# First attention of a four-layer kernel: the mask of half of the transposed score tiles goes from TensorE to VectorE

## The reference, cut to what matters

```python
q = apply_rope(proj(Wq, bq)) * Dh ** (-0.5)      # 16 heads of 16
k = apply_rope(proj(Wk, bk))
v = proj(Wv, bv)
scores = jnp.einsum('bhqd,bhkd->bhqk', q, k)
rel = idx[None, :] - idx[:, None]
blocked = (rel > 0) | (rel < -WINDOW)            # WINDOW = 128
scores = jnp.where(blocked[None, None], -jnp.inf, scores)
probs = jax.nn.softmax(scores, axis=-1)
out = jnp.einsum('bhqk,bhkd->bhqd', probs, v)
```

## Time and profile before

| | |
|---|---|
| median of 3 runs | 2595.47 us (2590.16 to 2601.94) |
| the profiled execution's own time | 2598.99 us |
| its span, first to last instruction | 2597.1 us |
| mean granted PE clock over the span | 0.945 |
| busy share of the span: PE, DVE, ACT, POOL | 85%, 54%, 38%, 35% |
| first attention, about | 60 to 1075 us of the span |

### The profile page before, as it was taken

The page is one execution under the profiler, slowest core; times in us unless marked ns, Lnnn a source line. Parts: engine busy times, 40 slices in busy tenths (PEclk is TensorE's granted clock), DMA queues, the critical chain, the costliest instruction groups (busy, mean ns, idle before and its releaser), DMA issues.

```text
span 2597.1 us, 42566 instructions
## 1 busy us (share of the span) xinstructions
PE 2202.2 (85%) x17140; PEld 1379.6 (53%) x17140; DVE 1411.1 (54%) x2526; ACT 994.3 (38%) x1450; POOL 898.7 (35%) x573
## 2 busy tenths in 40 slices
PE   3899999999999999588787879999678888888885
PEld 1444555555555455366565637766455555555553
DVE  2445555555555554346454535444467776777672
ACT  0133333333333333245444433333235554554443
POOL 4122222222222220003121221012438777777785
PEclk7799999999999999789889989999889999999997
DMA  5555555555555551455776661011454454436411
GB/s 132 103 113 116 107 115 114 107 108 113 114 111 117 111 110 39 149 195 196 239 268 232 241 206 49 17 65 49 150 144 115 116 159 133 129 101 172 112 48 49
DMA packets 226386, 328.86 MB, mean 127 GB/s; under 512 B 14368, under 2 KB 163984, under 8 KB 225936
## 3 DMA queue, kind: packets, MB, share of 16 engines
q1 hardware_dynamic: 219200, 321.56, 47.3%
q10 hardware_dynamic: 6992, 4.60, 0.6%
HBM read 197.53 MB, written 127.93 MB: 125 GB/s over the span
## 4 chain that ended last, share of the span: by engine, by line
PE 28%; DVE 11%; POOL 6%; DMA 6%; ACT 3%; issue 3%; SPq 2%; ACTq 0%; DVEq 0%; POOLq 0%
DVE l1f_rowmax L1811 4%; PE l1a_slot L1411 4%; POOL l1f_added L1688 4%; PE l1a_slot L1402 2%; POOL l1f_added L1690 2%; PE l0f_slot L1112 2%; PE l1a_slot L1453 2%; PE l1f_slot L1942 2%; PE l1f_slot L1933 2%; PE l0f_slot L1119 2%; DMA l0f_wide<-expert_outputs 2%; DMA l0f_x<-x 2%; PE l1f_os L1866 2%; DMA expert_outputs<-l0f_wide 1%; SPq L879 1%
## 5 line engine op out<-in xcount | busy, mean ns | idle before, releaser
L534 ACT ACTIVATE l0a_probs<-l0a_slot 128x1024 f32<-128x1024 f32 (+1 forms) x256 | 248.4, 971 | 336.2 <-PE l0a_slot L694 189.1
L591 DVE TENSOR_REDUCE l0a_rowmax<-l0a_slot 128x4 f32<-128x1024 f32 (+1 forms) x256 | 293.5, 1156 | 128.7 <-PE l0a_slot L704 125.8
L1760 ACT ACTIVATE l1f_probs<-l1f_slot 128x1024 f32<-128x1024 f32 x240 | 243.8, 1022 | 270.2 <-PE l1f_slot L1942 262.5
L1688 POOL TENSOR_TENSOR l1f_added<-l1f_probs 128x1024 f32<-128x1024 f32 x117 | 277.3, 2370 | 155.6 <-ACT l1f_probs L1760 155.6
L1811 DVE TENSOR_REDUCE l1f_rowmax<-l1f_slot 128x1 f32<-128x1024 f32 x240 | 287.5, 1217 | 65.7 <-PE l1f_slot L1933 65.1
L494 POOL TENSOR_TENSOR l0a_turned<-l0a_turned 128x512 f32<-128x512 f32 x32 | 40.7, 1272 | 557.0 <-DVE l0a_turned L577 557.0
L1942 PE MATMUL l1f_slot<-l1f_Qs,l1f_Ks 128*128 128x256 f32 x960 | 173.1, 305 | 37.2 <-DVE l1f_lo L1801 14.8
L1933 PE MATMUL l1f_slot<-l1f_Ks,l1f_Qs 96*128 96x512 f32 x480 | 179.0, 458 | 25.5 <-DVE l1f_rowmax L1811 18.7
L1942 PEld LDWEIGHTS l1f_slot<-l1f_Qs,l1f_Ks 128*128 128x128 f32 x960 | 146.5, 198 | 94.5 <-DVE l1f_rowmax L1811 31.9
L694 PE MATMUL l0a_slot<-l0a_mask,l0a_ident 128*128 128x512 bf16 (+1 forms) x512 | 150.3, 376 | 25.0 <-issue 22.6
L636 PE MATMUL l0a_O<-l0a_probs,l0a_V 128*32 128x128 f32 x3840 | 156.5, 279 | 10.4 <-issue 10.4
(11 more groups left out here) (196 smaller groups left out, 3987.9 us busy)
## 6 DMA issues: line engine op xcount, KB each, us to landing
expert_outputs<-l0f_wide SPq DMA_DIRECT2D x64, 512.0 KB, 3.4
l0f_wide<-expert_outputs SPq DMA_DIRECT2D x32, 1024.0 KB, 11.5
l0a_Qs<-qk_rows SPq DMA_DIRECT2D x96, 256.0 KB, 7.6
l0a_Ks<-qk_rows SPq DMA_DIRECT2D x96, 256.0 KB, 14.5
l1f_Ks<-kq_rows SPq DMA_DIRECT2D x48, 512.0 KB, 8.5
l0f_f<-in_dram SPq DMA_DIRECT2D x10, 2048.0 KB, 15.7
qk_rows<-l0a_hi SPq DMA_DIRECT2D x32, 512.0 KB, 2.8
qk_rows<-l0a_lo SPq DMA_DIRECT2D x32, 512.0 KB, 4.2
```

What stands on the lines that cost most here:

```text
L534: exp_ready.by(act.activation(probs[:, t % 2, HG * g:HG * g + HG, 0:reach, :], s[:, :, 0:reach, :], ACT.Exp, scale=SCALE))
L591: max_ready.by(dve.reduce_max(rowmax[:, t, :, 2 * g:2 * g + 2], s[:, :, :, first:2 * P], AX))
L1688: halved.by(pool.tensor_tensor(added[:, u, :], probs[:, 0, u, :], probs[:, 1, u, :], ALU.add))
L1760: exp_done.by(act.activation(probs[:, half, u - FIRST[b], :], s[:, :], ACT.Exp, scale=SCALE))
```

## The change

In tr steps with an odd g the two mask matmuls are left out: four score matmuls alone fill the slot. DVE gets a new part in these steps: as soon as the scores are there it adds the mask table to them, in place in PSUM, in one instruction over 128 x 1024 elements (128 x 512 for a sequence's last tile), and raises the new semaphore `masked`. ACT's exponential of these steps waits for `masked` besides the scores. The slot's reader is still the exponential. Tr steps with an even g and all nat steps stay as they were.

```diff
+        masked = signal("masked", BT * NHG // 2)
 ...
                 if kind == "tr":                       # ACT
                     t, g = i // NHG, i % NHG
                     s = by_pair(arrived(act, X, step)).rearrange("p s j a q -> p (s j) a q")
-
+                    if i % 2:
+                        masked.wait(act, X, i // 2 + 1)
 ...
+                if kind == "tr" and i % 2:             # DVE
+                    s = by_pair(arrived(dve, X, step)).rearrange("p s j a q -> p (s j) a q")
+                    reach = 1 if n and i // NHG == BT - 1 else 2
+                    visible_from = maskT[:, 0:reach, :].unsqueeze(1).broadcast_to([P, HG, reach, P])
+                    masked.by(dve.tensor_tensor(s[:, :, 0:reach, :], s[:, :, 0:reach, :], visible_from, ALU.add))
 ...
-                    mask_ends = bool(kind == "tr" and g % 2)
+                    masked_here = not (kind == "tr" and g % 2)
 ...
-                    if not mask_ends:
-                        add_mask()
+                    if masked_here:
+                        for half in range(2):
+                            mm(o[:, half, :, reach, :], ident16[:, :], table[:, reach, :].unsqueeze(1).broadcast_to([P, 2, wide, P]),
+                               start=True, stop=False, skip_group_check=True)
                     for j in range(2):
 ...
-                                      right[r, 2 * g + j, moving], start=mask_ends and not j, stop=not mask_ends,
+                                      right[r, 2 * g + j, moving], start=not masked_here, stop=True,
                                       skip_group_check=True, tile_position=(HALF * half, 0))
-                    if mask_ends:
-                        last = add_mask()
```

More of the change, by code:

```diff
@@ L399, in window_attention_layer @@
         stacked = {w: signal(f"stacked_{w}", 6, 16) for w in "qk"}
-        max_ready = signal("max_ready", BT * NHG); maxT_ready = signal("maxT_ready", BT)
+        masked = signal("masked", BT * NHG // 2); max_ready = signal("max_ready", BT * NHG); maxT_ready = signal("maxT_ready", BT)
         placed = [signal(f"placed{t}", BT, 16) for t in range(2)]
@@ L555, in _ @@
             dve.memset(ln.half[:, :], -0.5).then_inc(setup, 1)
-            for s in (turned_ready, v_ready, max_ready, maxT_ready, recip_ready, ao_ready, summed):
+            for s in (turned_ready, v_ready, masked, max_ready, maxT_ready, recip_ready, ao_ready, summed):
                 s.start(dve)
@@ L689, in piece @@
                     wide = reach.stop - reach.start
-                    mask_ends = bool(kind == "tr" and g % 2)
-                    def add_mask():
+                    masked_here = not (kind == "tr" and g % 2)
+                    if masked_here:
                         for half in range(2):
[L694 to L697, removed]
-                    if not mask_ends:
-                        add_mask()
+                            mm(o[:, half, :, reach, :], ident16[:, :], table[:, reach, :].unsqueeze(1).broadcast_to([P, 2, wide, P]),
+                               start=True, stop=False, skip_group_check=True)
                     for j in range(2):
```

## The result

The changed kernel takes 2698.8 us (median of 4 runs, 2690.98 to 2705.56) against 2597.01 us for the kernel before (also 4 runs): a ratio of 1.040, 95% interval 1.0358 to 1.0441, +102 us. The prediction said 2680 us with a range of 2636 to 2713, slower. The profiled execution took 2704.77 us, its span is 2702.8 us.

A forecast was written before the change was run, and what follows sets the result against it. PE, working in list order, was taken to set the pace, waiting only at unread slots. 2599.0 + 60.5 (waits) + 24 (clock) = 2683.5 us, given as a median of 2680 us; range 2636 to 2713 us.

The forecast's parts named there:

- The removed work: 128 odd tr steps lose two mask matmuls each on PE; at most 53 us saved.
- The addition's price: One DVE addition in PSUM takes 1.22 us, from its likeness to the residual sum; outer end 2.14 us.
- The rival of a slow write to PSUM: Every DVE addition takes 2.14 us, as PSUM reading and writing take turns; 2738 us; chance 0.09.
- The waits: PE waits for late exponentials: 1.90, 0.30, 1.54, 0.04 us in quarters 3, 0, 1, 2; 60.5 us over 16 blocks.
- The clock: In quarters 1 and 3, 6 of 10 new PE pauses halve the clock, 1.25 us each; 24 us.
- The first rival: Pauses in quarters 1 and 3 too short or well placed to lower the clock; waits only, 2656 us; chance 0.30.
- the prediction's other sum: All new pauses in quarters 1 and 3 lower the clock, costing 40 us in place of 24.
- PE's columns decide: Rival: DVE and ACT finish before PE returns, exponentials under about 0.4 us late in quarters 1, 3; 2543 us; chance 0.06.
- a wash: In quarters 1 and 3 the addition passes earlier DVE work for half the delay; near 2595 us; chance 0.05.

The follow-up runs named there:

- six-additions: Against the changed kernel, DVE adds the mask in all odd tr steps except tr1 of quarters 1 and 3, which have it on PE; 2601.89 us.
- picked: Against the changed kernel, DVE adds the mask only for tr3 of quarters 0 and 1 and tr1 of quarter 2; 2589.96 us.
- kernel with fillers: The changed kernel plus matmuls of no use in PE's pauses of quarters 0, 1 and 3, waits untouched; 2650.39 us.
- quarters 1 and 3 filled: The changed kernel plus matmuls of no use in PE's pauses of quarters 1 and 3 only; 2672.87 us.
- kernel with two additions: Against the changed kernel, DVE adds the mask only for tr1 of quarters 1 and 3, all others on PE; 2705.25 us.

## Why the prediction was right, by its steps

- *The removed work.* Right in that almost none of the 53 us shows, because PE waits behind the pairs. Where no wait follows it does show: 0.53 us for one pair, tr3 of quarter 1, in the six-additions and picked kernels. That is this pair's own spacing (567.25 to 567.78 in the kernel before, shown above); the 0.44 us taken for all pairs was read at another step.
- *The addition's price.* 1.22 us taken, 1.226 measured. The rival of a slow write to PSUM is out.
- *The waits.* 1.54 predicted and 1.46 measured in quarter 1, 1.90 and 1.90 in quarter 3, with the clock held up. Quarter 0: 0.30 and 0.24; quarter 2: 0.28 and 0.13 in one kind of blocks, -0.2 and -0.45 in the other. The sum was 60.5 us; 54.2 us were measured in the kernel with fillers. In quarter 0 the way there was not the one predicted: ACT's list was not full, tr3 moved by 0.39 us and not by 0.74 (4.42 us after tr1 instead of 4.03), and its missing mask gave 0.30 back and not 0.44.
- *The clock.* This is the term that was mis-sized: 24 us predicted, 48 measured (101.8 - 54.2). The step let 6 of 10 pauses bring the clock down, at 1.25 us each, in quarters 1 and 3 alone. In fact 14 of 16 pieces of quarter 1 and 13 of 15 of quarter 3 hold a stretch at half clock. It is 6.8 us long in most pieces of quarter 1, twice the 3.3 us of the step, and 3.4 in quarter 3; by the medians it costs 3.28 - 1.46 = 1.82 us and 3.07 - 1.90 = 1.17 us. Quarter 0, which the step did not price, lost to the clock in six blocks. Over all pieces the changed kernel lies above the kernel with all fillers by 25 us in quarter 1, 17 in 3, 8 in 0 and 2 in 2, in one trace of each; the medians of their runs lie 48 us apart. The first rival, waits without the clock, would have given 2656 us; it is what the kernel with all fillers gives, 2650 us, so the clock is what stands between that rival and the result. The Trainium skill's "TensorE: Matmul & The Clock Gate", section "A second HAM failure mode: psum-queue depth-cycling", says that short pauses between groups of matmuls bring the clock down and cost throughput, without a price. With every pause counted by that rule, the prediction's other sum was 40 us; the measured 48 lie nearer to it than to 24.
- *PE's columns decide*, and *a wash*: not borne out in the changed kernel. The first fails at the point named for it: tr1's exponential starts 1.82 us (quarter 3) and about 3 us (quarter 1) later than before, counted from its scores. The second asked that the addition pass the work ahead of it, and it passes none: in quarters 1 and 3 it starts when the last pass over k and the normalisation end.
- The end: 2680 predicted, 2698.8 measured. The 18.8 us are 24 us too little for the clock and 6 us too much for the waits, with 1.5 us from the median of the kernel before. Two errors of opposite sign make the forecast look closer than its clock term was.

## What to carry to other kernels

An operation given to a half idle engine cost here by what stood ahead of it in that engine's list and by who waited behind the reader, not by its share of the engine: 96 additions cost nothing that the kernel's time shows, and 32 cost about 100 us. Walk the slot ring step by step before moving work, and move it only where the next user of the slot is late anyway. And where a wait opens a pause in dense PE work, price the clock too; a few matmuls of no use in the pauses are a cheap way to find out what it costs.

## What the runs showed that was not expected

- The clock's share, 48 us, was almost as large as that of the waits, 54 us. Adding 16 matmuls of no use a block saved 26 us, and 21 a block 48 us.
- With quarters 1 and 3 filled, the clock fell in quarter 0 in eleven blocks of 16, where it had fallen in six with the same waits in the changed kernel. What decides whether pauses of that size bring it down is left open: a single pause of 2.4 us did not the earlier trace rows, and these shorter ones did in some blocks and not in others.
- Whether a step's mask goes first or last on PE has a price of its own: 0.35 us a block in quarter 0 of the kernel with two additions. No run has the kernel before with that order alone.
- The two DMA issues that ACT makes (1.28 us) stand on the path as soon as the activation ahead of them is late: moving them ahead of it, in the kernel with fillers, gained 13.7 us (2650.39 to 2636.66).
